# Row sums of a two-axis convolution in two 64x128 row tiles, units taken two by two, with changed places and load orders

## The reference

```python
x = x                                           # (8, 64, 64, 96)
xn = srms(x)                                    # x / (rms over the 96 channels + eps)
u = silu(xn @ u_w.T + u_b); v = silu(xn @ v_w.T + v_b)      # 288 channels each
out = tno(v, -3, rpe2) + tno(v, -2, rpe1)       # per channel: a 64x64 Toeplitz matrix along
                                                # columns, and another one along rows
return (u * out) @ o_w.T + o_b + x
# tno: coefficients from a small network (3 layers of 256) over 127 offsets, then a
# circular convolution of length 128 of which the first 64 outputs are kept
```

## Time and profile before

| | us |
|---|---|
| median of 3 runs | 815.77 (814.77 to 816.03) |
| the profiled execution's own time | 814.11 |
| its span | 812.3 |
| PE busy in the span | 749.5 (92%) |
| C0, 174 to 318: PE busy | 141.31 of 144 |
| C1, 546 to 690: PE busy | 142.41 of 144 |

### The profile page before, as it was taken

How to read it: one execution, slowest core, us unless ns; L and a number is a source line. 1 busy time by engine, 2 the same in 40 slices (tenths; PEclk the granted TensorE clock), 3 DMA queues, 4 the chain that set the end, 5 groups by cost and what they waited for, 6 DMA issues and landing times.

```text
span 812.3 us, 19208 instructions
## 1 busy us (share of the span) xinstructions
PE 749.5 (92%) x7148; PEld 672.2 (83%) x7148; DVE 470.2 (58%) x845; ACT 533.9 (66%) x866; POOL 282.6 (35%) x187
## 2 busy tenths in 40 slices
PE   0999997998999999899999999989999998987887
PEld 0999886988999998799999999979999998765655
DVE  6566542336898886444444454445455553776666
ACT  0566574775666666677777877746666666655554
POOL 4333333212212112655555555410000001966764
PEclk9999998999999999999999999989999999999999
DMA  9555554369889786488988888776555555688786
GB/s 209 159 156 156 156 134 138 160 199 215 187 193 200 160 187 191 144 272 272 270 271 262 266 275 271 231 202 144 133 134 131 136 134 185 200 250 248 247 262 193
DMA packets 132017, 161.11 MB, mean 198 GB/s; under 512 B 69484, under 2 KB 97132, under 8 KB 131948
## 3 DMA queue, kind: packets, MB, share of 16 engines
q1 hardware_dynamic: 131948, 160.15, 70.6%
HBM read 109.49 MB, written 50.63 MB: 197 GB/s over the span
## 4 chain that ended last, share of the span: by engine, by line
PE 75%; DMA 13%; DVE 4%; issue 2%; POOL 2%; SPq 2%; ACT 1%; ACTq 0%; DVEq 0%; POOLq 0%
PE ps L974 22%; PE ps L1049 15%; PE ps L1021 9%; PE ps L1034 9%; DMA out<-x_e 9%; PE ps L994 7%; PE ps L984 6%; PE ps L965 3%; DMA stage<-a_dram 2%; PE ps L997 1%; POOL u_in L504 1%; DMA u_dram<-u_in 1%; SPq L300 1%; PE ps L948 1%; DMA free_rows<-in_x 1%
## 5 line engine op out<-in xcount | busy, mean ns | idle before, releaser
L504 POOL TENSOR_TENSOR u_in<-u_in,v 128x1152 f32<-128x1152 f32 (+2 forms) x66 | 174.6, 2651 | 177.5 <-DMA u_in<-u_dram 161.0
L876 DVE TENSOR_TENSOR g<-ps,g 128x512 fp32r<-128x512 f32 (+1 forms) x192 | 125.7, 681 | 74.9 <-ACT g L571 45.8
L832 DVE COPY toepB<-stage 64x512 f32<-64x512 f32 x144 | 105.2, 730 | 80.1 <-PE ps L1049 72.6
L1049 PE MATMUL ps<-toepB,vt 128*128 128x128 f32 x1152 | 141.8, 277 | 0.9 <-POOL toepB L488 0.5
L1049 PEld LDWEIGHTS ps<-toepB,vt 128*128 128x128 f32 x1152 | 136.3, 194 | 1.4 <-POOL toepB L488 0.7
L974 PE MATMUL ps<-wu,xh 97*128 97x288 f32 x512 | 123.6, 307 | 2.1
L766 DVE TENSOR_TENSOR xl<-ps,xh 96x512 fp32r<-96x512 f32 x64 | 43.9, 687 | 140.5 <-ACT xh L544 140.5
L974 PE MATMUL ps<-wv,xh 97*128 97x288 f32 x512 | 120.8, 311 | 2.3 <-ACT u_in L548 1.3
L984 PE MATMUL ps<-ident,u_in 128*128 128x128 f32 (+1 forms) x768 | 102.2, 276 | 21.3 <-POOL u_in L504 20.3
L984 PEld LDWEIGHTS ps<-ident,u_in 128*128 128x128 f32 (+1 forms) x768 | 81.7, 127 | 36.8 <-DVE g L876 12.7
L548 ACT ACTIVATE v<-ps 128x576 f32 (+1 forms) x128 | 83.5, 652 | 38.2 <-PE ps L974 28.7
(11 more groups left out here) (79 smaller groups left out, 1006.5 us busy)
## 6 DMA issues: line engine op xcount, KB each, us to landing
stage<-a_dram SPq DMA_DIRECT2D x144, 256.0 KB, 4.3
u_in<-u_dram SPq DMA_DIRECT2D x64, 576.0 KB, 5.3
u_dram<-u_out SPq DMA_DIRECT2D x48, 576.0 KB, 3.3
x_e<-in_x_eT SPq DMA_DIRECT2D x64, 192.0 KB, 3.8
out<-x_e SPq DMA_DIRECT2D x64, 192.0 KB, 3.8
u_dram<-u_in SPq DMA_DIRECT2D x16, 576.0 KB, 2.8
x_n<-in_x SPq DMA_DIRECT2D x16, 384.0 KB, 5.4
xa<-in_x SPq DMA_DIRECT2D x64, 96.0 KB, 4.6
```

What stands on the lines that cost most here:

```text
L504: return nc.gpsimd.tensor_tensor(out=tile, in0=tile, in1=v[:, start // 2:end // 2, bass.ds(t * NB, NB)].rearrange("p c n e -> p n c e"), o ...
L832: nc.vector.tensor_copy(toepB[n % 2][rows, :, rows], stage[n % STAGES][rows, axis].rearrange("p k c -> p c k")[:, :, ::-1]).then_inc(toepB ...
L876: nc.vector.tensor_tensor(out=low, in0=ps[0:w, bank], in1=high.bitcast(f32), op=ALU.subtract).then_inc(gl_ready, 1)
L1049: last = nc.tensor.matmul(ps[:, SET_BANK[n % 2] + c // NB, (c % NB) * P:(c % NB + 1) * P], vt[n % 2][:, c], toepB[n % 2][:, c], start=Fals ...
```

## The change

The row sums are done with `toepB` of 64x64 for each channel: the upper 64 partitions of `vt` are the stationary operand of one matmul and the lower 64 that of another (64 rows by 128 columns each), each of which streams 64 columns and writes its own half of the output's columns. They are written alternately from the two halves, and into different banks, in two parts (`part`), with a new semaphore `rows_half` between the parts. `zero` and its semaphore go. PE takes the units two by two: columns(n), columns(n+1), the four row parts of the two units, T(n+2), T(n+3). ACT's code is written anew with the same order of copies: the sums of unit n, then the transposed unit n+2. DVE builds `toepB` with one copy in place of two. In stage A, chunk 4 of x gets a place of its own in `free_rows`, chunk 7 is loaded one chunk earlier and without a wait for `x_scaled`. In B1, SP issues the load of u, then the store, then the load of `x_e` for the present step in place of the next one.

```diff
-        x_late = [place(f"x_late{k}", [P, CHUNK_ROWS, E], V + offset) for k, offset in enumerate((36864, 13824, 0))]
+        x_late = [place(f"x_late{k}", [P, CHUNK_ROWS, E], V + offset) for k, offset in enumerate((0, 13824, 36864))]
...
-            return x_late[(c - FREE_CHUNKS) % 3][:]
+            if c == FREE_CHUNKS:
+
+                return free_rows[:, X_FREE:X_FREE + CHUNK_ROWS, 1, P - E:P]
+            return x_late[c - FREE_CHUNKS - 1][:]
...
-        toepB = [place(f"toepB{k}", [P, UNIT, P], V + (32768, 28672)[k]) for k in range(2)]
+        toepB = [place(f"toepB{k}", [P, UNIT, H], V + (32768, 28672)[k]) for k in range(2)]
...
             def phase_a(c, first, last):
-                if c + 3 < CHUNKS - 1:
+                if c + 3 < CHUNKS:
                     load_x_all(c + 3)
-                elif c + 2 == CHUNKS - 1:
-
-                    sp.wait_ge(x_scaled, CH * (c + 2 - 2))
-                    load_x_all(c + 2)
...
                             load_u(1, t + 3, r + 3)
-                        if not (first and r < CH - 1) and not (last and r == CH - 1):
-                            up = (r + 1) // CH
-                            sp.wait_ge(o_stored[1][(r + 1) % CH], 16 * c + 16 * up)
-                            load_xe(1, t + 1, r + 1)
                         if not first or r >= 2:
                             store_out(1, t - 2, r + 2)
+                        if not first:
+                            sp.wait_ge(o_stored[1][r], 16 * c)
+                            load_xe(1, t, r)
...
-                evacuate_vt(0)
+                for n in range(2):
+                    evacuate_vt(n)
                 for n in range(UNITS):
-                    if n:
-                        evacuate_y(n - 1)
-                    if n + 1 < UNITS:
-                        evacuate_vt(n + 1)
-                    elif half == 0:
+                    evacuate_y(n)
+                    if n + 2 < UNITS:
+                        evacuate_vt(n + 2)
+                    elif half == 0 and n == UNITS - 2:
                         high_x(STEPS, 0)
-                evacuate_y(UNITS - 1)
...
+                    for c in range(NB):
+                        for j in range(2):
+                            b, of = (j + part) % 2, slice(H * j, H * j + H)
+                            ch, at = NB * b + c, c * P + H * j
+                            last = nc.tensor.matmul(ps[:, SET_BANK[n % 2] + b, at:at + H], vt[n % 2][of, ch], toepB[n % 2][of, ch],
+                                                    start=False, stop=True, skip_group_check=True)
+                            if c == NB - 1:
+                                last.then_inc((rows_half, conv_done)[part], 1)
...
+                pe.wait_ge(silu_done, PAIRS * STEPS * (half + 1))
+                for n in range(2):
+                    transpose_v(n)
+                for n in range(0, UNITS, 2):
+                    for k in range(2):
+                        along_columns(n + k)
+                    if half == 0 and n + 2 == UNITS:
                         transpose_x(STEPS, 0)
-                    along_rows(n)
+                    for part in range(2):
+                        for k in range(2):
+                            along_rows(n + k, part)
+                    for k in range(2):
+                        if n + 2 + k < UNITS:
+                            transpose_v(n + 2 + k)
```

More of the change, by code:

```diff
@@ L90, in tno_kernel @@
         RSQ, RIN, W_RAW = RH + 2 * RC, RH + 4 * RC, RH + 6 * RC
-        assert W_RAW + 2 * NCH <= D // 2
+        X_FREE = W_RAW + 2 * NCH
+        assert X_FREE + CHUNK_ROWS <= D // 2
         def lw_row(n, o, layer, c):
@@ L201, in tno_kernel @@
         vt_transposed, vt_ready = sem("vt_transposed"), sem("vt_ready")
-        toep_zeroed = sem("toep_zeroed")
-        columns_done, conv_done, conv_out = sem("columns_done"), sem("conv_done"), sem("conv_out")
+        columns_done, rows_half = sem("columns_done"), sem("rows_half")
+        conv_done, conv_out = sem("conv_done"), sem("conv_out")
         RPE_LOADS = 1 + 2 * (RC + RC + 1)
@@ L313, in load_stage @@
                     sp.wait_ge(toepA_ready, UNITS * half + n - STAGES + 1)
-                    sp.wait_ge(toepB_ready, 2 * (UNITS * half + n - STAGES + 1))
+                    sp.wait_ge(toepB_ready, UNITS * half + n - STAGES + 1)
                 src = a_dram[0, n]
@@ L355, in phase_c @@
                     sp.wait_ge(toepA_ready, UNITS * half + n + 1)
-                    sp.wait_ge(toepB_ready, 2 * (UNITS * half + n + 1))
+                    sp.wait_ge(toepB_ready, UNITS * half + n + 1)
                     if k == 0:
@@ L484, in _ @@
                 phase_a(c, c == 0, c == CHUNKS - 1)
[L486 to L494, removed]
             for j in range(CHUNKS):
@@ L524, in _ @@
             chunks(pool, body0)
[L526 to L529, removed]
             open_b(1)
@@ L589, in evacuate_vt @@
                     act.wait_ge(vt_transposed, N + 1)
-                    wait(act, conv_done, N - 1)
+                    wait(act, conv_done, 2 * (N - 1))
                     nc.scalar.copy(vt[n % 2][:], ps[:, VT_BANK:VT_BANK + 2].rearrange("p b (c m) -> p (b c) m", m=P)
@@ L594, in evacuate_y @@
                 def evacuate_y(n):
-                    act.wait_ge(conv_done, UNITS * half + n + 1)
+                    act.wait_ge(conv_done, 2 * (UNITS * half + n + 1))
                     bank, pair, pairs = SET_BANK[n % 2], UNIT // 2 * n, UNIT // 4
@@ L824, in toeplitz @@
                     dve.wait_ge(stage_loaded[n % STAGES], 32 * ((UNITS // STAGES) * half + n // STAGES + 1))
[L825 to L835, removed]
+                    nc.vector.tensor_copy(
+                        (toepA, toepB)[axis][n % 2][:],
+                        stage[n % STAGES][:, axis].rearrange("p k c -> p c k")[:, :, ::-1]
+                    ).then_inc((toepA_ready, toepB_ready)[axis], 1)
                 toeplitz(0, 0)
@@ L858, in phase_c @@
                     if n + 2 < UNITS:
-                        dve.wait_ge(conv_done, UNITS * half + n + 1)
+                        dve.wait_ge(conv_done, 2 * (UNITS * half + n + 1))
                         toeplitz(1, n + 2)
@@ L865, in set_rows @@
             def set_rows(half, tiles):
-                dve.wait_ge(conv_done, UNITS * (half + 1))
+                dve.wait_ge(conv_done, 2 * UNITS * (half + 1))
                 for tile in tiles:
@@ L1038, in along_columns, with along_rows @@
                                 last.then_inc(columns_done, 1)
-                def along_rows(n):
+                def along_rows(n, part):
                     N = UNITS * half + n
[L1043 to L1062, removed]
-                        transpose_x(STEPS, 0)
-                    along_rows(n)
+                    if part == 0:
+                        pe.wait_ge(vt_ready, N + 1)
+                        pe.wait_ge(toepB_ready, N + 1)
+                        pe.wait_ge(columns_done, TILES * (N + 1))
+                    else:
+                        pe.wait_ge(rows_half, 2 * (N + 1))
```

## The result

The changed kernel takes 843.51 us (median of 4 runs, 840.02 to 846.96), the kernel before 815.27 beside it (812.87 to 816.03): a ratio of 1.035, interval 1.0303 to 1.04. It is slower. The profiled execution took 842.8 us, its span is 841.0, against 814.1 and 812.3.

A forecast was written before the change was run, and what follows sets the result against it. PE was taken to bound the Toeplitz stages, output stores and SP's load issue B1. 814.1 + 39.4 (pairs, C0 and C1) - 5.5 (x) - 13.5 (B1) = 834.5, forecast at 835 us; 8 in 10 range 818 to 849.

The forecast's parts named there:

- Row sums: Toeplitz stages: loads of 128 weight columns set the distance, so a unit's row sums stay at 1.8 us.
- first rival: Row sums at half their time: 64-row loads no limit, slot 0.056 us, pair 7.6 us, total 782; chance 0.11.
- The pair: Units two by two: second transposes wait for ACT's copy, 1.38 less 0.18 us, pair 9.24 in place of 8.04.
- C0's +21: Stage C0: 16 pairs +19.2 us, opening +0.3, end +1.5.
- C1: Stage C1: 17 pairs +20.4 us, opening -3, end +1.
- C1's opening -3: Second transposes fall into PE's idle time: -3 us, between -1.2 and -5 if PE then doesn't slow down.
- x: Stage A: earlier load of the last chunk of x ends POOL's wait; net -5.5 us, between -3 and -8.
- The wait that grows: Stage A: load's two issues precede a store of u that ACT and PE await; wait grows 1.6 to 3 us.
- the 2.5 us that were to come back from the low clock: Stage A: about half of PE's 5.20 us busy at clock 0.53 comes back, 2.5 us.
- B1: SP's wait for the store goes; step 3.25 us, near full DMA engines: -13.5 us, between -5 and -20.
- the forecast's own 823 to 846: Whole kernel: range of the forecast's main case, chance 0.76, from bounds of B1, x, C1's opening and the pairs.

The follow-up runs named there:

- weights_64: The changed kernel, each row matmul loading only 64 of its 128 weight columns, so half the row sums are left out; 781.7 us (one run).
- stream_32: The changed kernel, each row matmul streaming only 32 of its 64 columns, so half the row sums are left out; 901.01 us (one run).
- pairs_128: The kernel before with PE taking units two by two, row sums still 128x128 with zeros; 851.54 us, ratio 1.045.
- x_places: The kernel before with only the new places for x and the earlier last load of x; 811.61 us against 813.62, ratio 0.996.
- two_vt_banks: The changed kernel with transposes of odd units (from 3 on) in two PSUM banks of their own; 827.18 us against 813.62, ratio 1.014.
- act_order: two_vt_banks with ACT copying the sums of both units first, then both transposed units; 793.89 us against 813.32, ratio 0.976.
- best_act: best with ACT copying the sums of both units first, then both transposed units; 779.09 us, ratio 0.957.
- best: The kernel before (128x128 row sums) with B1's new order, places for x, units two by two and second PSUM banks; 815.65 us, ratio 1.001.
- tiles_single: The changed kernel with PE taking units one by one in the order of before; 822.69 us against 815.15, ratio 1.008.
- x_behind: The kernel before with B1's new order and places for x, last load of x behind its chunk's first store of u; 784.54 us, ratio 0.964.

## Why the prediction was right, and which terms were off

**Row sums: right.** A slot was taken at 0.11 us because the load keeps 128 columns. The pair's row sums take 3.72 us, weights_64 nearly halves their loads (3.65 to 2.02 us) and stream_32 leaves them at 3.65. The rows of a load made next to no difference: 32 slots in each tile in 3.72 us, 0.116 us each, with 64 rows; 32 loads in 3.77 us, 0.118 each, with 128 rows (pairs_128). With half the rows and half the streamed columns alone there was no gain; it came only when the weight columns, too, were 64, with 2.02 / 32 = 0.063 us a load in each tile. No run with 128 weight columns shows the first rival's slot of 0.056 us.

**The pair: right.** 9.24 us was predicted, 9.18 measured; the wait is 1.02 us of copy with the gaps beside it, and nothing of PE's fills it. pairs_128 shows the same wait without row tiles. C0's +21 is +21.7.

**C1: mis-sized, and one step failed.** The step "C1's opening -3" is wrong. Its second transposes do fall into PE's idle time, but PE then comes sooner to what unit 1 needs, and that isn't there. The column sums of unit 1 wait 1.06 us for `toepA`, and its row sums 1.81 us for `toepB`, which waits for the last store of u. What follows runs at a granted clock of 0.53. The prediction named the clock as a condition ("if PE then doesn't slow down"), and not these two waits. By the chain, the first pair, whose column sums start at 563.95, takes 580.00 - 563.95 = 16.05 us and the second 9.66, where a pair is 9.19: 7.3 lost. At the end the pair from 718.27 takes 12.10 and the last sums 6.80 in place of 5.71: 4.0 lost. In that pair PE stops for 0.76 us for a cause that the trace doesn't show, and the clock is low from 724 on. 17 pairs at 9.19, the last sums and ACT's copies of both units (737.17 to 740.88) would be 165.6 us; predicted was 148.2 + 18.4 = 166.6; measured is 176.9, and these two losses of 11.3 us are the difference. B0's +2.7 may be of the same kind, for it opens with 12 us at 0.57, where before had 1.00; it was not separated. The prediction reckoned with the low clock only where before had it.

**x: one term failed.** The wait that grows was put at 1.6 to 3 us, and it grew by 2.9 (ACT 2.18 to 5.10, PE 1.57 to 4.5). This fits the range, though the reason given, the 1.60 us of the load's issue in another place, doesn't: the issue took 4.29. What failed is the 2.5 us that were to come back from the low clock. The wait for x took its low stretch along (0.53 from 128 to 135), but PE's longer wait for the store has one behind it (0.57 from 116 to 124). -5.84 + 2.9 is -2.9, and -2.6 was measured. x_places, with the same wait but half of that low stretch in its profiled execution, is 5.1 earlier at this point, near the predicted 5.5.

**B1: mis-sized, on the good side.** The mechanism was right: the store's wait went. The step was taken as 3.25 us, "near the full engines"; it is 2.94, PE's own pace, and the stage gains 8.4 us more than predicted. The share of 0.80 at the old pace was no measure of what a step needs of the DMA engines: 0.80 x 3.94 = 3.15 us of engine time a step before, 0.96 x 2.94 = 2.82 after. Two slips of the working don't change this: 20 x 0.69 is 13.8, not 13.5, and two steps take 5.9 us at PE's 2.94, but 7.9 at the 3.94 that it calls today's pace.

The misses partly cancel: -8.4 in B1 against +10.3 in C1, +2.9 in A, +2.7 in B0 and +0.7 in C0, together +8.2 on a sum of +20.4, which is the span's +28.7 but for rounding. The 843.5 us lie inside the range, 8.5 above the forecast. That they lie so near is in part luck: without B1's surplus the time would be near 852, outside the forecast's own 823 to 846.

## What to carry to other kernels

Ask first whether a matmul costs its streamed columns or its weight load. Here, with 32 to 128 streamed columns and 128 weight columns, it was the load (3.69 us a pair with 32 streamed columns, 3.72 with 64, 3.77 with 128): splitting the contraction into row tiles doubled the instructions and left the time. Before two like steps are put behind one another, look at what the second needs of the first through another engine (here a PSUM bank that ACT must empty), and at the whole queue of that engine, since two_vt_banks removed one wait and met the next. Work that is moved into idle time gains only if what stands behind it is ready by then: in C1's opening it wasn't. A load that is issued early stands ahead of something: price its issue at the new place, and what waits behind it.

## What was unexpected of the hardware

- stream_32 does the same instructions as the changed kernel with half of the streamed columns in the row sums, and in its one execution the granted clock in C0 averaged 0.77 in place of 1.00; the time rose from 843.5 to 901.0 us. weights_64, whose PE idles more (105.33 busy of 129 us), kept 1.00 in the same place. Why was not settled.
- With the same order of PE's units, the kernel with row tiles had the lower mean clock in every execution of two pairs of kernels: 0.973 to 0.980 (the changed kernel, four) against 0.985 to 0.989 (pairs_128, four), and 0.974 to 0.984 (act_order, four) against 0.988 to 0.991 (best_act, four). pairs_128 and the changed kernel also differ in stages A and B1. Between two_vt_banks (0.983 to 0.985) and best (0.982 to 0.994) the two overlap, and in tiles_single, units one by one, it was 0.985 to 0.990, about as before. So a lower clock went with the row tiles in the order of pairs, not in each kernel to the same extent; what in them brings it is open.
- The DMA engines reached a share of 0.96 and 307 GB/s over 90 us of B1, with PE still setting the pace.
- The same two issues of a load on SP took 1.60 us in one place and 4.29 in another, right behind two issues of a store (a_dram) that took 4.13. Whatever stood first behind that store was slow to issue: the store of u took 3.38 us there before and 2.74 in x_behind, and 0.98 with the load of x between.
